# Layer 0's causal mask: a GpSimd select on the probabilities in place of a mask product in the score bank

## The reference, cut to what matters

```python
mask = jnp.triu(jnp.full((T, T), -jnp.inf, dtype=x.dtype), k=1)[None, None]
s1 = jnp.einsum('bhtd,bhsd->bhts', q1, k1) * scale + mask
a1 = jax.nn.softmax(s1, axis=-1)
...
diff = a1 - lam * a2
out = jnp.einsum('bhts,bhsd->bhtd', diff, v)
```

## Time and profile before

| what | value |
|---|---|
| time, median of 3 runs | 567.65 us (566.27 to 568.22) |
| span of the profiled execution (the page gives it no other time) | 567.5 us |
| PE busy | 469.4 us, 83% of the span |
| DVE busy | 356.8 us, 63% |
| ACT busy | 244.4 us, 43% |
| POOL busy | 201.6 us, 36% |
| mean granted TensorE clock | 0.924 of 2.4 GHz |

### The profile page before, as it was taken

One profiled execution on the slowest core, in us unless ns is written; L12 is line 12 of the kernel. 1 busy time (PEld: TensorE's weight loads), 2 busy tenths in 40 slices (PEclk: granted clock), 3 DMA queues, 4 the chain that ended last, 5 costly groups with the idle time before them and its releaser, 6 DMA issues.

```text
span 567.5 us, 11368 instructions
## 1 busy us (share of the span) xinstructions
PE 469.4 (83%) x4080; PEld 322.9 (57%) x4080; DVE 356.8 (63%) x887; ACT 244.4 (43%) x459; POOL 201.6 (36%) x276
## 2 busy tenths in 40 slices
PE   3377499998999997799999999766788897789961
PEld 1254376565566663377776776444565665567540
DVE  3888356998998775135431338887877777741335
ACT  1052157375466655643353323225153553754212
POOL 2432030326486604005000047136435565520324
PEclk9778789998999998999999999988879888999985
DMA  8897400000210100233332253006100013000204
GB/s 275 269 388 217 99 1 3 5 2 3 75 59 23 39 4 3 56 113 102 103 107 72 74 186 102 2 1 241 57 2 11 11 49 104 3 3 1 72 25 147
DMA packets 28831, 44.11 MB, mean 78 GB/s; under 512 B 5729, under 2 KB 25057, under 8 KB 27489
## 3 DMA queue, kind: packets, MB, share of 16 engines
q1 hardware_dynamic: 26473, 37.09, 20.4%
q0 software_dynamic: 2304, 6.29, 3.5%
HBM read 28.13 MB, written 14.94 MB: 76 GB/s over the span
## 4 chain that ended last, share of the span: by engine, by line
PE 58%; DVE 25%; issue 5%; POOL 4%; DMA 4%; ACT 3%; SPq 0%; POOLq 0%; DVEq 0%; ACTq 0%
PE bank L933 8%; PE bank L955 6%; PE bank L739 6%; PE bank L828 5%; DVE work L1431 5%; PE bank L727 4%; PE bank L835 4%; PE bank L763 4%; PE bank L856 3%; DMA work<-work 3%; PE bank L759 3%; PE bank L878 3%; PE bank L787 3%; PE bank L784 2%; PE bank L940 2%
## 5 line engine op out<-in xcount | busy, mean ns | idle before, releaser
L1020 ACT ACTIVATE work<-bank 96x1024 bf16<-96x1024 bf16 (+5 forms) x187 | 107.7, 586 | 115.8 <-PE bank L739 49.7
L1431 DVE TENSOR_REDUCE work<-bank 128x4 f32<-128x512 f32 (+1 forms) x144 | 96.9, 686 | 47.7 <-PE bank L763 45.7
L1062 ACT ACTIVATE work<-bank 128x512 f32<-128x512 f32 x144 | 84.0, 596 | 77.9 <-PE bank L787 47.7
L739 PE MATMUL bank<-identb,work 128*96 128x128 bf16 x576 | 52.5, 248 | 23.7 <-DVE work L1359 7.8
L1188 POOL COPY work<-work 128x1024 bf16<-128x1024 bf16 (+1 forms) x16 | 19.5, 1218 | 123.8 <-DVE work L1415 123.8
L739 PEld LDWEIGHTS bank<-identb,work 128*96 128x96 bf16 x576 | 46.9, 146 | 28.3 <-issue 19.6
L727 PE MATMUL bank<-wqkv,xnT 128*128 128x512 f32 (+1 forms) x128 | 55.0, 562 | 3.4 <-ACT xnT L1020 1.5
L1738 DVE TENSOR_TENSOR work<-work,bank 128x176 f32<-128x176 f32 x47 | 15.8, 336 | 59.5 <-ACT work L1115 59.3
L759 PE MATMUL bank<-neg_ts,identb 128*128 128x512 bf16 (+1 forms) x144 | 48.3, 335 | 5.7 <-DVE work L1431 4.4
L835 PE MATMUL bank<-work,cst 128*32 128x256 f32 (+1 forms) x768 | 50.6, 333 | 0.0
L763 PE MATMUL bank<-work 96*128 96x256 bf16 (+1 forms) x320 | 49.0, 258 | 0.0
(11 more groups left out here) (204 smaller groups left out, 843.4 us busy)
## 6 DMA issues: line engine op xcount, KB each, us to landing
moe<-w_in SPq DMA_DIRECT2D x9, 1056.0 KB, 11.0
x_slots<-wo SPq DMA_DIRECT2D x41, 128.0 KB, 1.8
work<-x_slots SPq DMA_DIRECT2D x31, 128.0 KB, 2.2
y_slots<-work SPq DMA_DIRECT2D x31, 128.0 KB, 1.7
moe<-f1a_in SPq DMA_DIRECT2D x1, 2048.0 KB, 8.7
moe<-f1b_in SPq DMA_DIRECT2D x1, 2048.0 KB, 13.2
moe<-x_slots SPq DMA_DIRECT2D x1, 1280.0 KB, 6.2
work<-x_in SPq DMA_DIRECT2D x4, 256.0 KB, 5.8
```

Of the source, the lines that this page charges most:

```text
L739: mm = nc.tensor.transpose(bfv(a.pj.bank(key))[0:STACK, u, :], stack[:, 8 * g + u].rearrange("p s d -> p (s d)"), identb[:, :])
L1020: return nc.scalar.activation(dst, src, ACT.Copy)
L1062: nc.scalar.activation(pT[at % 6], a.st.bank(w)[:, :], ACT.Exp, scale=SCALE)\
L1431: nc.vector.tensor_reduce(here[:, first:first + len(ms), half], a.s.bank((b, q))[:, :].rearrange("p (m s) -> p m s", s=n), AX_X, ALU.max, ...
```

## The change

In layer 0 the mask product L784 is gone and the score product alone fills the bank. POOL does a select on each `pT` tile of layer 0 as well, and `value` waits for it (`a.cut`) and no longer for ACT alone.

```diff
                 if a.n == 0:
-                    nc.tensor.matmul(view[:, :, 0:P], neg_ts[:, :],
-                                     identb[:, :].unsqueeze(1).to_broadcast([P, len(ms), P]),
-                                     start=True, stop=False, skip_group_check=True)
                     nc.tensor.matmul(view, qk[0:DEEP, a.maps + j, keys * P:keys * P + P],
-                                     qk[0:DEEP, ms[0]:ms[-1] + 1, t0:t0 + n], start=False, stop=True,
-                                     skip_group_check=True).then_inc(a.st.full, 1)
+                                     qk[0:DEEP, ms[0]:ms[-1] + 1, t0:t0 + n], start=True, stop=True)\
+                        .then_inc(a.st.full, 1)
                     return
...
-                pe.wait_ge(*(a.st.emptied((b, j, 2)) if a.n == 0 else (a.cut, a.st.at[(b, j, 2)] + 1)))
+                pe.wait_ge(a.cut, a.st.at[(b, j, 2)] + 1)
...
-                    elif kind == "exp" and a.n == 1:
+                    elif kind == "exp":
                         maps, n = (2, SEQ) if w[2] < 2 else (4, P)
                         pool.wait_ge(*a.st.emptied(w))
```

## The result

| | time, median | runs | span of the profiled execution | mean granted clock |
|---|---|---|---|---|
| before | 566.97 us (566.27 to 568.22) | 4 | 567.5 us | 0.924 |
| after | 588.54 us (587.17 to 590.62) | 4 | 588.9 us | 0.900 |

The ratio is 1.0359, 95% interval 1.0329 to 1.039: the change makes the kernel 3.6% slower. The sign was forecast; the size was not. It is 21.4 us by the spans and was put at 8.5, and the median lies half a microsecond above the range.

The account below looks back on a forecast made before the run. PE was taken to pace from 80 to 100 us, DVE (or both in turn) from 100, and POOL to become the bound in beats 75 to 99. Terms -2.5 + 4 + 6 + 0 + 1 = +8.5 on 567.5 gave 576 us, range 567 to 588.

Parts of the forecast that it names:

- beats 75 to 99: Layer 0's attention behind the first send: POOL becomes the bound, 8.4 us idle for 12.5 us of selects; +6 us.
- The mask's price: Layer 0's 96 mask products: removing them gives PE at most 14.4 us, and only where PE paces.
- Beats 34 to 60: Some 68 to 124 us: PE gains from missing masks until 100 us, then DVE bounds; -2.5 us, bounds 0 and 3.5 gained.
- Beats 61 to 72: Selects behind `mid` delay `value` (1,1), then DVE's maxima and `value` (1,3); +4 us, bounds 1.9 and 5.4.
- Beats 100 to 117: Four spaced `norm` steps on POOL, each unit a ring with `max` steps: no gain; 0, bounds -2.7 and +2.
- Beats 118 to 131: No `max` steps: bare ring of score, exponential, select and `value`, 3.35 us instead of 3.23; +1 us, bounds 0 and 1.5.
- Behind the attention: Everything after layer 0's attention starts from its last `value` and just shifts with it; 0.
- Faster: Rival: selects fall into POOL's idle time, no `value` waits, PE keeps its gain; 559 us, chance 0.13 including a 537 us case.
- No change: Rival: lower bounds hold in both POOL stretches and PE gains 2.5 and 2.7 us; 568 us, chance 0.10.
- The clock rival: PE's new waits of some 3 to 5 us bring stretches at the lower clock; 585 us, chance 0.15.
- POOL without idle time from the first send on for some 50 us: Sign named as showing the forecast right: POOL continuously busy in layer 0's attention after the first send.
- selects beside DVE would run longer: Beats 75 to 99: wide selects slowed by DVE's two-SBUF-operand work; 2.7 us more if all 8, kept for the range.

Follow-up runs that it names:

- E3a: The kernel before plus 96 selects of the same shapes on a scratch tile, waiting for nothing of layer 0 and waited for by nobody: 574.23 us, ratio 1.0108.
- E3b: The kernel before plus 96 scratch-tile selects that each wait for their exponential, while `value` waits for no select: 580.04 us, ratio 1.0189.
- E2: The changed kernel with the mask product L784 put back, so it has both mask and select: 593.36 us, ratio 1.0455 to the kernel before.
- E9: The changed kernel with layer 0's `value` steps one beat later (values=5, not 4): 578.65 us, ratio 1.0158 to the kernel before.
- E11: The kernel before, with mask product and no select in layer 0, its `value` step one beat later: 571.63 us, ratio 1.0048.
- E8: The changed kernel with selects only in batches 0 and 3 and the mask product in 1 and 2: 573.53 us, ratio 1.0071 to the kernel before.
- E4: The changed kernel with most sends moved behind beat 96: 596.87 us, ratio 1.0462 to the kernel before.
- E1: The kernel before without the mask product L784 and without any select, so layer 0 is unmasked: 564.97 us, ratio 0.9938.
- E10: The changed kernel with `value` one beat later and at most one other POOL step between two selects: 590.49 us, ratio 1.0335 to the kernel before.
- E5: The changed kernel with POOL's order rewritten, at most one other step between two selects: 585.32 us, ratio 1.0271 to the kernel before.

## Why the prediction was right or wrong

**The step that failed** is the term for beats 75 to 99: +6 us, bounds 4.1 and 12.5; it measured +13.3, which is 7.3 of the 12.9 us that the sum lacks. It compared room with work: 8.4 us of idle time on POOL for 12.5 us of selects, and took a value near the lower end because "inputs for which POOL waited are there when it comes late". That treats POOL as a server with a load. Its first step, `value` (1,6) 2.7 us late, was already short: it came 9.9 us late, 5.1 more than `value` (1,5). Load is E3a, 2.0 us in this stretch, and E3b with its late inputs 4.7: a forecast from occupancy would have been near right for a select that nobody waits for. The rest, 7.7 us between E3b and E2, comes with the wait of `value` (in E2 PE stands still 6.4 us longer, 10.8 and not 4.4, and its work takes 1.3 us more), and it comes from a ring: a select waits for an exponential, the exponential for PE's scores, the scores stand behind a `value`, and that `value` waits for an earlier select, which stands behind sends, power, `high` or `mid`. In this ring the idle time of each engine is where it waits for the others, and the selects didn't fill it: POOL kept 11.7 of 12.9 us. E9 shows the ring by slackening it, one beat for 8.8 us of this stretch (E11: the beat by itself gains nothing there); E8 shows it by taking it away; E4 shows that it isn't load, with 21.6 us of idle time on POOL and the same loss. The step also overlooked that POOL had been running ahead of its beats, and that the selects of 73 to 75 end that: the 3.6 us ahead of the first send. And it left the clock to a rival: up to 4.0 us of this stretch, below.

**The mask's price** (at most 14.4 us, not the page's 30.7) holds as a bound: E1 gets 6.8 us back between (0,0) and (3,7), 3.5 in the time.

**Beats 34 to 60: -2.5 forecast, +0.6 measured** between (0,0) and (1,0), 3.1 of the 12.9 us. By (0,5) the changed kernel had gained 1.6 us, and E1 2.0; the saving is real and a little smaller. It is then lost at one place, the projection L727 of a later tile. PE's timeline in the changed kernel:

```profile
108.82 3.64 PE L727 MATMUL bank<-wqkv,xnT 128*128 128x512 f32 x4 [1.96 <-DVE small L1542]
```

And in E2, which has the same selects and keeps the mask product:

```profile
108.63 1.96 PE L727 MATMUL bank<-wqkv,xnT 128*128 128x512 f32 x4 [1.41 <-DVE small L1545]
```

PE, done sooner, waits longer for DVE (1.96 us and not 1.41), and behind the longer wait runs the projection at the lower clock, as a window of 2 us in the changed kernel shows:

```profile
110.00:112.00 2.00, 2.00 (x3) 0.52 (x3) 1.82 (x4) 0.00 (x0) 1.93 (x4) 0.50 0.00 0
```

E1, without any select, has the same wait of 1.96 us and the four matmuls take 3.25 us, so POOL has no part in it. The sum counted "nothing more" from 100 us on, and there was a loss.

**Beats 61 to 72: +4 forecast, +3.6 measured.** The first steps are as put: `mid` ends at 132.94 us, the select behind it at 133.64 (132.3 forecast), `value` (1,1) waits 5.92 us (5.4 forecast). Then PE works at the lower clock, 0.50 in the window of 134 to 139 us (`value` (1,1) has 1.08 where it had 0.64), and the transpose of the row maxima, L800 here, is 5.9 us late and not 2.5:

```profile
138.53 0.31 PE L800 MATMUL bank<-identb,work 128*96 128x128 bf16 x1
```

`value` (1,3) is 6.5 us late (4.4 forecast), 1.2 of it from the beats ahead, and then 1.7 us come back. That the sum of the stretch is near its term is in part luck.

**Beats 100 to 117: 0 forecast, 0.0 measured. Beats 118 to 131: +1 forecast, +1.5 measured.** The ring of the last units is bare there, and the starts of two successive ones, 250.14 and 253.51 us, are 3.37 us apart where 3.35 was worked out. **Behind the attention** the forecast had 0; it is +1.9, and ahead of (0,0) +0.6: within the spread of those columns, and not settled.

**The rivals.** Faster (559 us) is excluded twice: the select of beat 63 came after PE, and E1, whose select costs nothing, is at 565. No change fails with the sum. The clock rival's 585 us came nearest, but for a reason that carries only a part. E1 and the changed kernel have the same matmuls on PE; from `value` (1,5) to `value` (2,5), E1 first (columns as in the earlier trace rows):

```profile
153.53:195.80 42.27, 38.96 (x479) 25.83 (x478) 38.08 (x91) 28.10 (x48) 31.49 (x37) 1.00 0.14 47
...
157.42:213.99 56.57, 42.93 (x480) 28.11 (x479) 38.15 (x91) 28.34 (x49) 44.87 (x63) 0.91 0.12 40
```

The changed kernel takes 14.3 us longer. For 10.3 us of that PE stands still (13.6 us and not 3.3), and 4.0 us more go into the same matmuls at a clock of 0.91 and not 1.00. Those 4.0 us are the most that the clock cost directly here, since busy time also grows where matmuls overlap less. The changed kernel's low stretches here begin at 167.0 us, in the wait of 5.04 us, and at 194.3 us, behind that of 2.89. E10 shows that the clock can carry most of a loss: 7.5 of 9.1 us there.

Of what would show it, `value`'s waits, longest behind `mid` and behind sends, came as written. "POOL without idle time from the first send on for some 50 us" was wrong, and is the plainest sign of the failed step. That selects beside DVE would run longer, kept for the range, did not come but for three of the 96 (0.89 to 1.16 us): in 60 to 262 us the narrow ones took 419 ns and the wide 667 in the mean, less than in the earlier trace rows.

```profile
L1178 POOL TENSOR_SCALAR_AFFINE_SELECT work<-work 128x256 f32<-128x256 f32 x64 | 26.4, 419 | 42.0 <-ACT work L1059 38.5 <-DVE slot L1569 2.3
L1178 POOL TENSOR_SCALAR_AFFINE_SELECT work<-work 128x512 f32<-128x512 f32 x32 | 21.4, 667 | 31.0 <-ACT work L1059 30.7
```

## What to carry to other kernels

When work moves to an engine with idle time, don't weigh the work against the idle time: ask whether the engine waits for the one that will wait for it. If so, its idle time may be no room, as here, and the price is what stands ahead of the moved instruction in its queue, again and again around the ring; look for work that the engine did ahead of its beat and no longer can. What helped is distance: one beat more between producer and consumer took the loss from 3.6% to 1.6%. A different order in the queue mostly moved the wait (E5 2.7%, E4 4.6%, and E10 3.4% with the added beat). To tell waits from a slower clock, compare PE's busy time over the same matmuls: a list of waits doesn't show the clock's part.

## What the runs showed of the hardware

A saving on TensorE can come with a cost by the clock. The four matmuls of L727 took 1.95 or 1.96 us behind a wait of 1.40 or 1.41 us (the kernel before, E2, E3a and E3b) and 2.58 to 3.64 us behind a wait of 1.96 us (the changed kernel, E1, E4, E5 and E8); the rows show the lower level, 0.50, in those five and not in those four. That the length of the wait decides is not shown: in E9 the level is 0.50 in the window of 107 to 109 us with no such wait ahead of that projection.

The lower level's price can be read where PE has the same matmuls: 39.49 us of work at 1.00 (E9) and 46.99 at 0.85 (E10). And 30.7 us of busy time in the page's group of L784 were worth 3.5 us of the kernel's time.
